# A routed FFN whose expert tiles are gathered through an inverse slot map, and whose shared pieces stand four ahead of the loop and four behind it

## The chip, the cores and the metric
One core of one Trainium2 chip. The metric is the device time of one execution in microseconds. Engines: TensorE (PE), VectorE (DVE), ScalarE (ACT), GpSimd (POOL), SyncE (SP).

## The reference
x has 2 batches of 512 tokens of 512 values. Three layers, each on a layer norm of x:
```
x = x + 0.5 * ffn(layernorm(x))
x = x + attention(layernorm(x))     # 32 heads, 8 key/value heads, head size 128, causal
x = x + 0.5 * ffn(layernorm(x))     # the same weights
ffn(h):
  shared  = (silu(h @ Wg.T) * (h @ Wu.T)) @ Wd.T                  # inner size 512
  probs   = softmax(h @ gate.T)                                   # 16 experts
  w1, w2  = the two largest, divided by their sum
  routed  = w1 * expert_e1(h) + w2 * expert_e2(h)                 # each a gated FFN of inner size 128
  return shared + routed
```

## The kernel before
Everything is float32. A product is split into a high and a low part, high x high + low x high + high x low (PARTS), each float32r; ACT writes the high parts by a copy, DVE or POOL the low parts by a subtraction. The program is written out by hand for each engine, with semaphores between them; each engine works through its list in order.

The tokens are 8 tiles of 128 (TT), two halves of 4. One FFN (`feed_forward(n)`, n = 0 and 1) runs in this order on PE: transposes of the normed half 0 (`turn_norm`), gate/up of shared piece 0, transposes of half 1, `router`, gate/up 1, down 0, `rank`, then for s from 2 to BEFORE-1 gate/up s and down s-1, the transpose of the first expert tile, down BEFORE-1, the loop over expert tiles (`routed`), and the pieces from BEFORE on. The shared FFN is cut into 4 slices of its inner size times 2 halves of the tokens: SLOTS = 8 pieces; a piece is 24 matmuls of gate/up and 12 of down. A slice's weights arrive in `raw_w` and are cut into `wgu` and `wdn`. Down s writes the banks 4 to 7, and `add_down(s)` on DVE adds them to x; a bank is free again only then.

Routing before. DVE's `router` takes softmax, the eight largest and their indices and forms one-hot rows (`hot`, `chosen`). PE's `rank` counts with `below` and `ones` how many tokens ahead chose the same expert. DVE's `place` works out the row of each (token, choice) in a list sorted by expert, each expert padded to whole tiles of 128 (`rows`), and the expert of each of the TILES = 31 tiles, packed six at a time into the integers `tile_w`; it ends with `rows` of the semaphores. Then POOL scatters the 8 tiles of normed tokens twice, 16 indirect DMAs, into `x_rows` in HBM, which was cleared before by a DMA of 31 tiles; SP waits for `scattered` and loads tile after tile (`load_tile`). The experts' weights (16 of 768 KB) are loaded in two groups of eight, ordered among the tile loads; ACT's step waits for the part of them that it needs (`there`).

The loop takes four tiles per iteration, the first iteration and the last written out. `places` reads `tile_w` and works out where in `experts` the weights of six tiles lie. A step j, engine by engine:
- PE: transposes x of tile j+1; transposes `ht` of tile j-1; gate/up of tile j in 12 matmuls, the first three from `tfront`, the other nine from `tback` (wait for `back_lo`); down of tile j-1.
- ACT: `tback_hi` of tile j+1 (768 elements), hT of j-1, `xT_hi`, `tfront_hi` (256 elements), silu of tile j.
- DVE: `xT_lo` and `tfront_lo` of tile j+1, the product `ht` of tile j, the copy of y of tile j-1.
- POOL: `tback_lo` of tile j+1 (768 elements).
- SP: loads tile j+4, stores y of tile j-1 into `y_rows`.

Behind the loop POOL gathers 16 times from `y_rows` into `yg` (two choices for each token tile), and DVE's `combine` adds them with their weights to x: combine 0 between the pieces 6 and 7, combine 2 behind piece 7, combines 4 and 6 behind `add_down(7)`. After the first FFN come `raw_q` and the cuts of attention's weights (`first_cuts` on ACT and POOL: wks, wvs, wqs 0 to 3) and the layer norm of half 0, whose chain on DVE goes `statistics`, ACT's root, `newt` (three steps), `rstd`, the scaling of `xn`; only then PE can transpose and project. After the second FFN the tiles of x are stored, each when it is finished.

## Time and profile before

| | us |
|---|---|
| median of 3 runs | 1210.75 |
| lowest, highest | 1207.58, 1211.01 |
| the profiled execution | 1207.59 |
| its span | 1205.9 |
| first FFN, from the span's start to attention's first projection | 219.8 |
| attention | 784.9 |
| second FFN's loop over expert tiles, and what follows it | 95.2, 33.5 |

The page gives busy time of an engine as a share of the span; a window gives it for a stretch; the chain of waits follows the last instruction back to what released it; a timeline lists instructions in order of time, with the idle time ahead of each and what ended it in square brackets.

### The profile page before, as it was taken

The page shows a single profiled execution, that of the slowest core. Times are in us where ns is not written, and L with a number is a line of the kernel's source. Part 1 is how long each engine was busy: PE and PEld are TensorE (multiplying, and loading weights), DVE is VectorE, ACT ScalarE, POOL GpSimd, SP SyncE. Part 2 cuts the span into 40 slices and gives each one's busy share as a digit, 9 for nine tenths or more (in the row PEclk, how much of TensorE's full clock was granted, in tenths as well). Part 3 has the DMA queues.
Part 4 walks back from the last instruction along what each step waited for, and adds up shares of the span by engine and source line. Part 5 has one row for each costly group of instructions (what it writes and reads, how often), then busy time and mean ns, then how long its engine had stood idle before and what let it go on. Part 6 is the DMA issues. An engine that isn't in the chain of part 4 may idle for free.

```text
span 1205.9 us, 20326 instructions
## 1 busy us (share of the span) xinstructions
PE 1130.7 (94%) x6110; PEld 943.2 (78%) x6111; DVE 701.6 (58%) x1836; ACT 557.6 (46%) x1352; POOL 473.4 (39%) x485
## 2 busy tenths in 40 slices
PE   5989996789999999999999999999999989989994
PEld 4777774678888888888888888888888876877773
DVE  5767776855455545454545454554554556867766
ACT  3336662346435445344544443534553543246650
POOL 1266556116315324323432532531532410365545
PEclk9999998889999999999999999999999999999998
DMA  9986547101101010010010110010100007744546
GB/s 356 346 303 212 161 148 244 53 1 36 53 2 36 9 44 0 35 52 0 35 52 0 35 52 0 35 52 0 35 1 1 1 15 287 301 141 157 160 144 209
DMA packets 38603, 114.62 MB, mean 95 GB/s; under 512 B 4384, under 2 KB 4384, under 8 KB 36512
## 3 DMA queue, kind: packets, MB, share of 16 engines
q1 hardware_dynamic: 33440, 97.30, 22.4%
q0 software_dynamic: 5120, 16.78, 4.1%
q8 instruction: 23, 0.38, 0.1%
q14 instruction: 20, 0.16, 0.0%
HBM read 79.20 MB, written 34.87 MB: 95 GB/s over the span
## 4 chain that ended last, share of the span: by engine, by line
PE 86%; DVE 4%; DMA 3%; issue 2%; ACT 2%; POOL 2%; DVEq 0%; SPq 0%; ACTq 0%; POOLq 0%
PE bank L1221 22%; PE bank L1286 15%; PE bank L1252 10%; PE bank L1298 10%; PE bank L1200 7%; PE bank L1127 6%; PE bank L1234 6%; PE bank L1208 4%; PE bank L1143 2%; POOL yg L484 2%; PE bank L1169 2%; PE bank L1188 1%; PE bank L1100 1%; DMA raw_w<-in_ffn_w 1%; PE bank L1088 1%
## 5 line engine op out<-in xcount | busy, mean ns | idle before, releaser
L498 POOL TENSOR_TENSOR scores<-scores,pinv 128x512 f32<-128x512 f32 (+3 forms) x256 | 176.7, 723 | 378.9 <-DVE pinv L996 378.9
L651 ACT ACTIVATE pT_hi<-bank 128x384 fp32r<-128x384 f32 (+1 forms) x192 | 93.9, 524 | 137.1 <-PE bank L1234 137.1
L450 POOL TENSOR_TENSOR tback_lo<-experts,tback_hi 128x768 fp32r<-128x768 f32 x62 | 115.0, 1857 | 74.4 <-ACT tback_hi L593 73.4
L676 ACT ACTIVATE oT_hi<-bank 128x512 fp32r<-128x512 f32 x64 | 38.3, 599 | 221.5 <-PE bank L1298 221.5
L664 ACT ACTIVATE scores<-scores,nmax 128x512 f32<-128x512 f32 (+3 forms) x256 | 140.3, 557 | 0.3 <-DVE nmax L986 0.3
L966 DVE TENSOR_TENSOR pT_lo<-bank,pT_hi 128x384 fp32r<-128x384 f32 (+1 forms) x192 | 109.5, 598 | 46.9 <-ACT pT_hi L651 46.8
L986 DVE CUSTOM_DVE_ANT_0 scores<-bank,causal 128x512 f32<-128x512 f32 (+3 forms) x256 | 112.2, 486 | 2.2 <-issue 0.2
L970 DVE TENSOR_TENSOR oT_lo<-bank,oT_hi 128x512 fp32r<-128x512 f32 x64 | 44.3, 692 | 112.7 <-ACT oT_hi L676 112.7
L1286 PE MATMUL bank<-wds_hi,oT_hi 128*128 128x512 f32 x256 | 105.5, 412 | 1.4 <-DVE oT_lo L970 1.4
L1221 PE MATMUL bank<-xnT_hi,wqs_hi 128*128 128x512 f32 x256 | 106.7, 417 | 0.0
L1221 PE MATMUL bank<-xnT_lo,wqs_hi 128*128 128x512 f32 x256 | 101.8, 398 | 0.0
L1221 PE MATMUL bank<-xnT_hi,wqs_lo 128*128 128x512 f32 x256 | 101.2, 395 | 0.0
L1286 PE MATMUL bank<-wds_hi,oT_lo 128*128 128x512 f32 x256 | 100.3, 392 | 0.0
L1286 PE MATMUL bank<-wds_lo,oT_hi 128*128 128x512 f32 x256 | 100.0, 391 | 0.0
L1234 PE MATMUL bank<-ident,scores 128*128 128x128 f32 x640 | 90.8, 272 | 2.3 <-DVE pT_lo L966 2.3
L1252 PE MATMUL bank<-kT_hi,qT_hi 128*128 128x512 f32 (+3 forms) x256 | 84.8, 331 | 1.9 <-DVE qT_lo L970 1.9
L1234 PEld LDWEIGHTS bank<-ident,scores 128*128 128x128 f32 x640 | 75.3, 140 | 11.3 <-DVE pT_lo L966 2.8
L1252 PE MATMUL bank<-kT_lo,qT_hi 128*128 128x512 f32 (+3 forms) x256 | 82.6, 323 | 0.0
L1298 PE MATMUL bank<-pT_hi,vv_lo 128*128 128x512 f32 (+3 forms) x256 | 82.6, 323 | 0.0
L1298 PE MATMUL bank<-pT_lo,vv_hi 128*128 128x512 f32 (+3 forms) x256 | 82.3, 321 | 0.0
L1252 PE MATMUL bank<-kT_hi,qT_lo 128*128 128x512 f32 (+3 forms) x256 | 82.2, 321 | 0.0
L1006 DVE TENSOR_TENSOR x<-bank,x 128x512 f32<-128x512 f32 x64 | 44.1, 691 | 64.8 <-PE bank L1286 64.8
(192 smaller groups left out, 2854.0 us busy)
## 6 DMA issues: line engine op xcount, KB each, us to landing
experts<-in_ffn_w SPq DMA_DIRECT2D x32, 768.0 KB, 10.1
xn<-x_rows SPq DMA_DIRECT2D x62, 256.0 KB, 2.7
y_rows<-xn SPq DMA_DIRECT2D x62, 256.0 KB, 2.0
raw_q<-in_wq SPq DMA_DIRECT2D x8, 1024.0 KB, 5.3
raw_d<-in_wd SPq DMA_DIRECT2D x8, 1024.0 KB, 4.8
x_rows<-experts SPq DMA_DIRECT2D x1, 7936.0 KB, 30.0
raw_w<-in_ffn_w SPq DMA_DIRECT2D x8, 768.0 KB, 7.6
raw_kv<-in_wkv SPq DMA_DIRECT2D x8, 512.0 KB, 3.3
```

What stands on the lines that cost most here:

```text
L450: nc.gpsimd.tensor_tensor(tback[par][1][:], experts[:, bass.ds(at + FRONT, GU - FRONT)], tback[par][0][:].bitcast(F32), ALU.subtract).then ...
L498: nc.gpsimd.tensor_tensor(s, s, pinv[k % 2][:, i:i + 1].to_broadcast([P, P * (i + 1)]), ALU.mult).then_inc(att.normed, 1)
L651: nc.scalar.activation(pT[0][:, lo_col:hi_col], bank[b][:, 0:hi_col - lo_col], ACT.Copy).then_inc(att.t_hi, 1)
L664: nc.scalar.activation(s, s, ACT.Exp, bias=nmax[par][:, i:i + 1], scale=-1.0, accum_out=psumr[par][:, i:i + 1]).then_inc(att.exp, 1)
L966: nc.vector.tensor_tensor(pT[1][:, lo_col:hi_col], bank[b][:, 0:hi_col - lo_col], pT[0][:, lo_col:hi_col].bitcast(F32), ALU.subtract).then ...
L986: nc.vector.tensor_tensor_reduce(sp_[par][:, TRI[i]:TRI[i + 1]], bank[bk][:, c:c + w], causal[:, 512 - w:512], -SCORE_SCALE, 3.0e38, ALU.a ...
L1200: last = nc.tensor.matmul(bank[par][:, 0:2 * INTER], xT[par][a][:, c, :], piece[b][:, start:start + FRONT], start=(i == 0), stop=(i == 3 * ...
L1221: last = nc.tensor.matmul(into[:], w[a][:, c, :], xnT[z][:, c, b * SEQ:(b + 1) * SEQ], start=(m == 0), stop=(m == 3 * HC - 1))
L1234: last = nc.tensor.transpose(bank[b][:, at + (i - j) * P:at + (i - j + 1) * P], sp_[par][:, TRI[i] + j * P:TRI[i] + (j + 1) * P], ident[:])
L1252: last = nc.tensor.matmul(bank[bk][:, c:c + P * (i + 1)], qT[a][:, i * P:(i + 1) * P], kT[b][z][:, 0:P * (i + 1)], start=(m == 0), stop=(m ...
L1286: last = nc.tensor.matmul(o_bank(u)[:], oT[ob][h][a][:, tile * P:(tile + 1) * P], wds[h][z][:], start=(m == 0), stop=(m == 3 * G - 1))
L1298: last = nc.tensor.matmul(bank[1][:, j * P:SEQ], vv[bu][a][:, j, :], pT[z][:, COL[j]:COL[j] + SEQ - j * P], start=(j == 0 and m == 0), sto ...
```

## The change
No scatter and no `x_rows`. SP stores the normed tokens as they are into `xn_rows` (two stores of four tiles). `place` ends with two sets of one-hot matrices: `token_hot` (which of the 31 tiles a (token, choice) goes to, which POOL multiplies by the token's number) and `lane_hot` (which lane in the tile). PE's `invert` multiplies them, 16 matmuls of 32 columns, and one more packs the experts of the tiles; DVE's `map_slots` copies the result: `slots`, the token number for each lane of each tile, and `tile_w`. POOL then gathers each expert tile from `xn_rows` with one indirect DMA, four ahead of the loop and then one in each step.

The router's matmuls take high and low gate weights together (2 x 16 columns of weights), 16 in place of 24; the softmax goes, since only the ratio exp(second - first) is needed. `rank` stands ahead of down 0 and uses bank 1. The low part of gate/up slice 1 goes from DVE to POOL. BEFORE is 4 in place of 6. ACT waits once for all 16 experts. In the loop DVE takes the first third of `tback_lo` (`middle`), POOL the rest; POOL's steps are written out. Behind the loop the combines stand ahead of pieces 6 and 7, two pairs each, and the norm of attention waits only for `add_down(6)`; `raw_q` waits for the second pair of gathers. Shared slice 3 is loaded once all gate/up of the loop are done.

```diff
-BEFORE = 6
+BEFORE = 4
@@ SP
+            def store_norm(n, h):
+                part = slice(HALF * h, HALF * h + HALF)
+                sp.wait_ge(norm[2 * n].mul, HALF * (h + 1))
+                sp.dma_start(xn_rows.rearrange("(t p) h -> p t h", p=P)[:, part, :],
+                             xn[:, part, :]).then_inc(route[n].stored, 16)
...
+                load_experts(0, 2)
+                store_norm(n, 0)
+                load_experts(2, 5)
+                store_norm(n, 1)
+                load_shared(n, 2)
+                load_experts(5, NEXP)
                 for k in range(4):
                     store_tile(n, 0, k)
...
+                sp.wait_ge(moe[n].gu_mm, TILES)
+                load_shared(n, 3)
...
-            sp.wait_ge(gathered[HALF - 1], 2 * 16)
+            sp.wait_ge(gathered[HALF // 2 - 1], 4 * 16)
@@ POOL
                 def back(par, at, count):
                     pool.wait_ge(tile_part.back_hi, base + count)
-                    nc.gpsimd.tensor_tensor(tback[par][1][:], experts[:, bass.ds(at + FRONT, GU - FRONT)],
-                                            tback[par][0][:].bitcast(F32),
+                    nc.gpsimd.tensor_tensor(tback[par][1][:, FRONT:], experts[:, bass.ds(at + 2 * FRONT, GU - 2 * FRONT)],
+                                            tback[par][0][:, FRONT:].bitcast(F32),
                                             ALU.subtract).then_inc(tile_part.back_lo, 1)
+                def gather(j):
+                    wait(pool, moe[n].x_mm, j - RING + 1)
+                    nc.gpsimd.indirect_dma_start(
+                        out=xn[:, j % RING, :], out_offset=None, in_=xn_rows,
+                        in_offset=bass.IndirectOffsetOnAxis(ap=slots[:, j:j + 1], axis=0)).then_inc(tile_in[j % RING], 16)
+                pool.wait_ge(route[n].slots, 1)
+                pool.wait_ge(route[n].stored, 2 * 16)
+                for j in range(RING):
+                    gather(j)
+                low_gu(n, BEFORE // 2)
+                pool.wait_ge(route[n].table, 1)
+                back(0, places(pool, 0)[1], 1)
+                low_dn(n, BEFORE // 2)
+                for it in range(TILES // 4 + 1):
+                    at = places(pool, it)
+                    for k in range(4):
+                        j = 4 * it + k
+                        if j + 1 < TILES:
+                            back(1 - k % 2, at[k + 2], j + 2)
+                        if j + RING < TILES:
+                            gather(j + RING)
...
+                low_gu(n, 1)
+                pool.wait_ge(route[n].tokens, 1)
+                flat = token_hot[:].rearrange("p (m t) j -> p m t j", m=2)
+                nc.gpsimd.tensor_tensor(flat, flat.bitcast(F32),
+                                        token[:].unsqueeze(1).unsqueeze(3).to_broadcast([P, 2, TT, TILES + 1]),
+                                        ALU.mult).then_inc(route[n].tokens, 1)
@@ ACT
-                act.wait_ge(route[n].rows, 1)
-                at, there = places(act, 0, loads=True)
-                back(0, at[1], there[1])
-                act.wait_ge(ffn[n].dn_lo, NSH - 1)
+                act.wait_ge(route[n].table, 1)
+                act.wait_ge(m.weights, 16 * NEXP)
+                at = places(act, 0)
+                back(0, at[1])
+                act.wait_ge(ffn[n].dn_lo, BEFORE // 2)
@@ DVE, norm of attention
-                    dve.wait_ge(moe[0].added, 2 * HALF * (h + 1))
+                    dve.wait_ge(ffn[0].added, HALF * (SLOTS - 1 + h))
@@ DVE, place
+                row = rowf[:].rearrange("p m t -> p (m t)")
+                then(nc.vector.tensor_scalar(tile_of[:], row, 1.0 / P, -(P - 1) / (2.0 * P), ALU.mult, ALU.add))
+                then(nc.vector.tensor_scalar(tile_of[:], tile_of[:], ROUNDED, -ROUNDED, ALU.add, ALU.add))
+                dve.wait_ge(s.stored, 2 * 16)
+                nc.vector.tensor_tensor(token_hot[:], counts[:, 0:TILES + 1].unsqueeze(1).to_broadcast([P, 2 * TT, TILES + 1]),
+                                        tile_of[:].unsqueeze(2).to_broadcast([P, 2 * TT, TILES + 1]),
+                                        ALU.is_equal).then_inc(s.tokens, 1)
+                then(nc.vector.scalar_tensor_tensor(out=lane_of[:], in0=tile_of[:], scalar=-float(P), in1=row,
+                                                    op0=ALU.mult, op1=ALU.add))
+                for m in range(2):
+                    nc.vector.tensor_tensor(lane_hot[m][:], counts[:].unsqueeze(1).to_broadcast([P, TT, P]),
+                                            lane_of[:, TT * m:TT * (m + 1)].unsqueeze(2).to_broadcast([P, TT, P]),
+                                            ALU.is_equal).then_inc(s.lanes, 1)
...
+            def map_slots(n, then):
+                s = route[n]
+                dve.wait_ge(s.mapped, 1)
+                nc.vector.tensor_copy(slots[:], bank[1][:, 256:256 + TILES + 1]).then_inc(s.slots, 1)
+                dve.wait_ge(s.exp, 1)
+                then(nc.vector.tensor_scalar(tsum[:], ratio[:], 2.0, 2.0, ALU.mult, ALU.add))
+                then(nc.vector.reciprocal(wtop[:, :, 0], tsum[:]))
+                then(nc.vector.tensor_tensor(wtop[:, :, 1], wtop[:, :, 0], ratio[:], ALU.mult))
+                nc.vector.tensor_copy(tile_w[:], bank[1][0:1, 384:384 + WORDS]).then_inc(s.table, 1)
@@ DVE, loop
+                def middle(par, at, count):
+                    dve.wait_ge(tile_part.back_hi, base + count)
+                    nc.vector.tensor_tensor(tback[par][1][:, 0:FRONT], experts[:, bass.ds(at + FRONT, FRONT)],
+                                            tback[par][0][:, 0:FRONT].bitcast(F32),
+                                            ALU.subtract).then_inc(tile_part.middle_lo, 1)
...
                     if exists(j, 0, TILES - 2):
+                        middle(1 - par, at[k + 2], j + 2)
                         turned(1 - par, j + 2)
                         front(at[k + 2], j + 2)
@@ DVE, feed_forward
                 then = router(n)
-                shared(n, 1, 2)
+                multiply(n, 1)
                 place(n, then)
-                shared(n, 2, BEFORE)
+                shared(n, 1, 2, multiplied=True)
+                shared(n, 2, 3)
+                map_slots(n, then)
+                shared(n, 3, BEFORE)
                 routed(n)
-                shared(n, BEFORE, SLOTS - 1)
+                shared(n, BEFORE, SLOTS - 2)
                 combine(n, 0)
+                combine(n, 2)
+                shared(n, SLOTS - 2, SLOTS - 1)
+                combine(n, 4)
+                combine(n, 6)
                 shared(n, SLOTS - 1, SLOTS)
-                combine(n, 2)
...
             add_down(0, SLOTS - 1)
-            combine(0, 4)
-            combine(0, 6)
@@ PE
                 wait(pe, f.mul, s - 1)
+                if s == 3:
+                    pe.wait_ge(route[n].table, 1)
...
+            def invert(n):
+                s = route[n]
+                pe.wait_ge(s.tokens, 2)
+                for m in range(2):
+                    pe.wait_ge(s.lanes, m + 1)
+                    for t in range(TT):
+                        i = TT * m + t
+                        last = nc.tensor.matmul(bank[1][:, 256:256 + TILES + 1], lane_hot[m][:, t, :], token_hot[:, i, :],
+                                                start=(i == 0), stop=(i == 2 * TT - 1), skip_group_check=True)
+                pe.wait_ge(s.expert_of, 1)
+                pe.wait_ge(consts.packing, RING + 2)
+                nc.tensor.matmul(bank[1][0:1, 384:384 + WORDS], tilef[:], packing[:], start=True, stop=True,
+                                 skip_group_check=True).then_inc(s.mapped, 1)
...
                 gate_up(n, 1)
+                rank(n)
                 down(n, 0)
-                rank(n)
                 for s in range(2, BEFORE):
                     gate_up(n, s)
+                    if s == 2:
+                        invert(n)
                     down(n, s - 1)
```

## Rows read from the trace of the kernel before

**Rows 1.** The page, span and engines: busy us (share of the span), instructions
```profile
span 1205.9 us, 20326 instructions
...
PE 1130.7 (94%) x6110; PEld 943.2 (78%) x6111; DVE 701.6 (58%) x1836; ACT 557.6 (46%) x1352; POOL 473.4 (39%) x485
```

**Rows 2.** Windows: stretch, length, busy us of each engine, granted clock, DMA share, GB/s
```profile
87.20:181.15 93.95, 89.57 (x564) 68.75 (x564) 67.52 (x118) 62.22 (x147) 52.58 (x29) 1.00 0.53 181
202.40:219.80 17.40, 3.67 (x16) 3.27 (x16) 15.53 (x23) 6.07 (x10) 10.96 (x11) 0.61 0.66 254
1005.00:1022.60 17.60, 15.10 (x84) 10.25 (x82) 13.18 (x30) 9.01 (x16) 2.35 (x1) 1.00 0.96 386
1172.40:1205.90 33.50, 17.49 (x74) 13.39 (x72) 19.09 (x29) 2.46 (x4) 16.21 (x16) 0.84 0.64 204
```

**Rows 3.** Chain of waits, first FFN ahead of the loop: start us, us, what
```profile
26.46 5.58 PE bank L1100 x24
...
33.12 5.80 PE bank L1127 x24
...
41.90 1.69 PE bank L1158 x16
...
49.29 2.75 PE bank L1143 x12
```

**Rows 4.** Timeline of DVE, routing: start, us, line, instruction, output<-input, count, [idle before]
```profile
38.96 0.29 DVE L826 TENSOR_TENSOR chosen<-hot 128x128 f32<-128x128 f32 x1
...
40.10 1.23 DVE L868 TENSOR_TENSOR wgu_lo<-raw_w,wgu_hi 128x1024 fp32r<-128x1024 f32 x1 [0.26 <-ACT wgu_hi L550]
...
41.85 2.48 DVE L887 SCALAR_TENSOR_TENSOR x<-bank,x 128x512 f32<-128x512 f32 x4
...
45.63 0.42 DVE L843 TENSOR_REDUCE ahead<-wide 128x16 f32<-128x256 f32 x1
...
47.95 0.71 DVE L853 TENSOR_TENSOR wide<-counts,upto 1x544 f32<-1x544 f32 x1
```

**Rows 5.** Timeline of all engines, one iteration of the first loop
```profile
137.01 0.33 PE L1188 MATMUL bank<-ident,ht 128*128 128x128 f32 x1 [0.59 <-DVE ht L931]
...
138.78 0.41 DVE L921 TENSOR_TENSOR tfront_lo<-experts,tfront_hi 128x256 fp32r<-128x256 f32 x1
...
146.09 0.85 ACT L593 ACTIVATE tback_hi<-experts 128x768 fp32r x1 [1.01 <-issue]
...
147.25 1.82 POOL L450 TENSOR_TENSOR tback_lo<-experts,tback_hi 128x768 fp32r<-128x768 f32 x1 [2.05 <-ACT tback_hi L593]
...
148.23 1.12 DVE L921 TENSOR_TENSOR tfront_lo<-experts,tfront_hi 128x256 fp32r<-128x256 f32 x1
...
149.60 0.33 PE L1188 MATMUL bank<-ident,ht 128*128 128x128 f32 x1 [0.60 <-DVE ht L931]
```

**Rows 6.** Timeline of all engines, from the first loop's end towards attention
```profile
185.61 0.98 POOL L484 DMA_INDIRECT yg<-y_rows,rows  x1 [9.29 <-DMA y_rows<-xn]
...
186.90 0.96 POOL L484 DMA_INDIRECT yg<-y_rows,rows  x1 [0.30 <-issue]
...
199.36 2.73 DVE L959 SCALAR_TENSOR_TENSOR x<-yg,wtop,x 128x512 f32<-128x512 f32 x4
...
206.00 7.42 DVE L768 TENSOR_TENSOR newt<-root 128x4 f32<-128x4 f32 x1 [0.71 <-ACT root L526]
...
208.48 4.91 POOL L505 TENSOR_TENSOR wqs_lo<-raw_q,wqs_hi 128x512 fp32r<-128x512 f32 x4
...
214.72 3.67 PE L1088 MATMUL bank<-ident,xn 128*128 128x128 f32 x16 [12.35 <-DVE xn L773]
```

**Rows 7.** Windows of PE alone: stretch, length, busy us, granted clock, DMA share, GB/s
```profile
198.50:202.40 3.90, 3.87 (x10) 0.56 0.92 322
246.00:256.50 10.50, 8.44 (x30) 0.52 0.00 0
1189.20:1192.20 3.00, 2.99 (x12) 1.00 0.83 231
```

292 lines of the change are left out of this document (115 added, 177 removed).

## The prediction

> **What bounds the kernel now.** The page comes first: TensorE (PE) is busy 1130.7 of a span of 1205.9 us [rows 1], so only about 75 us can be won without taking matmuls away. The windows say where PE is not busy: little in the attention stage, 16.0 us in the tail behind the last expert tile, 13.7 us in the passage from the first FFN to attention, 4.4 us in the first loop over expert tiles [rows 2]. The chain of waits gives the price of each piece of PE work [rows 3], the timelines of the engines the order behind each idle spot [rows 4 to 6]. Attention's code is untouched and priced at nothing. The kernel has two FFNs, so every FFN term counts twice. The sum is made against the profiled execution, 1207.59 us (span 1205.9 and 1.7 around it); the median of the three runs lies 3.2 us above it. About 0.3% (3.6 us) is what a measurement of this kernel can tell from no change.
>
> I follow the path in three parts: up to the end of the last gate/up before the loop, the loop, and what follows it.
>
> **Part 1, routing against fewer pieces.** A piece costs PE 5.6 (gate/up) plus 2.75 (down), 8.35 us [rows 3]. BEFORE 6 to 4 takes two out of this part: -16.7. The routing then has to fit into less work, and it grows.
> - Router: 24 matmuls in 5.58 become 16, 1.9 less [rows 3]; but two ACT copies of 0.6 that queue behind the first piece's activation gate the transposes, so I count 1.1: gate/up 1 starts at 32.0, not 33.1.
> - Router chain on DVE: the softmax and its small steps go, an addition of the halves comes; `chosen`, now ready at 39.2 [rows 4], comes 3 us earlier and before PE needs it. Hidden.
> - `rank` now stands ahead of down 0 and starts when gate/up 1 ends, 37.8, and takes 1.7 to 1.9 [rows 3]: DVE's `place` starts at 39.75. At 39.0 POOL starts the low part of gate/up 1, 2.4 us, formerly DVE's 1.23 [rows 4]. Its second and third instructions find it busy. How that goes the loop shows: `tfront_lo`, both inputs in SBUF, takes 0.41 alone and 1.12 when POOL's `tback_lo` is under way, ending 0.28 after it [rows 5]; one of four elements took 7.42, as long as POOL's cuts behind one another [rows 6]. So `place` stands until 41.35: 1.2 lost.
> - Then by the nearest rows (0.2 for a small one, 0.42 to 0.46 for 256 elements, 0.71 for 544, 1.23 for 1024 [rows 4]): 3.1 to `tile_of`, 0.7 for `token_hot`, then two `lane_hot` of 1.23 on DVE and POOL's multiply of 512 elements, 1.23 as its cuts in [rows 6], all needing both inputs from SBUF and so one after another: 3.7. Last 0.8 for the expert of each tile. End about 49.7, ranging 48.4 (the 0.8 beside POOL) to 51.
> - PE after `rank`: down 0 and gate/up 2, done at 48.05. `invert` is 17 small matmuls; `rank`'s 16 take 1.69 [rows 3]; half of them wait for the lanes. It ends at 49.9, and down 1 waits further for the low part and the first add, to 51.0: about 3 us lost with `invert` itself. Down 1 ends at 53.75.
> - Gate/up 3 waits for `table`, which DVE writes only after the low part (0.6), add 0 (2.48 [rows 4]), multiply 2, an ACT copy, low part 2 (2.0 in all), add 1 (2.48), low down (0.6) and `map_slots` (1.0): 49.7 + 9.1 = 58.8. PE is idle 5.05 us from 53.75. This is the largest new wait. Gate/up 3 ends at 64.4, against 74.4 for gate/up 5 now: **-10.0** per FFN instead of -16.7.
> - Clock: after pauses the granted clock falls. The row after a 2.1 us pause shows 0.56, one in attention's start 0.52 over 10.5 us, half speed being 1.2 GHz; after 2.3 us at 1186.9 it stayed 1.00 [rows 7]. The transposes behind 12.35 us of idleness took 3.67 [rows 6]. Five idle microseconds behind one more lie nearer the first kind: I take 4 us of matmuls at half speed, **+2.0** per FFN; bounds 0 and 5 (the 10.5 us stretch).
> - DMA: gone are the 7.9 MB clear and 16 scatters per FFN, come two stores of 1 MB. ACT now waits for all 16 experts, the last 11 issued near 29 us behind DVE's first low down. The row of such loads shows 386 GB/s [rows 2]; 12 loads of 0.79 MB take 24.5 us and end near 55, needed at 66 (second FFN: 11 us of room). SP stands on `stored` sources and that low part meanwhile; queued behind it are only loads with room. Cost nothing; without that room every late microsecond would count.
>
> **Part 2, the loop.** One iteration of four tiles takes 12.59 us, from one PE transpose of `ht` to the same four later [rows 5]. It is not PE's 2.84 per tile that sets it but this ring: ACT `tback_hi`, POOL `tback_lo` (1.82), DVE `tfront_lo` 0.28 behind POOL, DVE `ht`, PE, and ACT again; two tiles take 5.9 us, and once per iteration ACT stands 1.01 for the registers of `places`, 0.84 more than else [rows 5]: 5.9 + 5.9 + 0.8 = 12.6.
> The change takes a third from POOL's piece (1.82 to 1.23), gives DVE `middle` (0.41), and puts a gather behind POOL's piece, 0.96 and 0.30 of issue [rows 6]. POOL per tile: 0.3 + 1.23 + 0.3 + 1.0, 2.83 to 2.9; with `places` 0.47 per iteration, 11.9. Everything hangs on who takes the port first. POOL's piece used to start 0.15 to 0.3 us before DVE was free; now the gather keeps POOL until after DVE has started `middle`, and that repeats itself, since the loop is entered so. PE then sees 2.85 per tile and 3.45 at the boundary: 12.0. 25 intervals at 0.15 less (the last four have no gather): -3.7, of which I keep **-3.0** per FFN, for gathers that take 1.44 at times. Bounds: -5 (PE's own rate), +6 (POOL first: `middle` waits for it, two tiles 6.25 and 13.3 per iteration). The loop's entry is taken as now, -0.25. The gathers themselves are issued three tiles ahead and hidden.
>
> **Part 3, behind the loop.** PE has four pieces, 33.5 us, in place of two, 16.7. POOL's 16 gathers begin 4.4 us behind the loop's end and take 1.26 each [rows 6], landed by 27: now covered. But DVE is late. From the multiply of piece 5 (11.3 us behind the loop's end): low gate/up and add 4 to 16.55, two pairs of combines (2.73 per four [rows 6]) to 21.95, piece 6 and add 5 to 26.95, two more pairs to 32.35, piece 7's multiply, ACT copy and low part to 34.35, add 6 to 36.75. Down 7 can start at 34.95, PE having been idle 4.2 us. Second FFN: add 7 ends at 39.2 (full clock) to 40.9 (half), then 2.45 to the end as now: 41.65 to 43.35, I take 42.5. Now it is 33.5 [rows 2]: **+9.0**.
> First FFN: statistics from add 6, root 3.2 later, 40.3 us; ACT then cuts `wqs` 1 to 3 and POOL follows at 40.85 with three cuts of 1.23. The chain `newt`... `rstd` needs 0.8 and its last step, both inputs in SBUF, comes at 40.9. In the row now `newt` stood until the last of six cuts [rows 6], so I let it stand until 44.6, then 5.7 to the first projection as now, half-speed transposes included (0.7 behind the end of `newt` to 219.8 [rows 2, 6]), and 0.1 for the rest of the chain. 50.4 against 38.65 (181.15 to 219.8): **+11.7**; bounds +8.1 (it slips through) and +12.2.
> Here a page bears on it. The Trainium skill, SBUF — State Buffer, Who interferes with whom, says that a DVE instruction with two SBUF inputs contends with a GpSimd one that reads SBUF, and that `tensor_scalar` in a 2-port mode contends too. The first half the trace shows, 7.42 us [rows 6]; for the second no row has POOL beside the scaling of `xn`. By that rule +11.7 would hold even if `rstd` slipped through, without it +8.1 would be reached.
>
> **Sum.** First FFN: -10.0 + 2.0 - 0.25 - 3.0 + 11.7 = +0.45. Second: -10.0 + 2.0 - 0.25 - 3.0 + 9.0 = -2.25. Together -1.8: 1207.6 - 1.8 = 1205.8 on the profiled execution's level, 1209 on the median's.
>
> **Rivals.**
> A, more is hidden (0.27): pauses do not lower the clock (-4 to -5), the `wqs` cuts let `rstd` by (-3.6), the loop runs at PE's rate (-4). All: -14; two of them: 1197 to 1205. For it: 2.3 us left the clock alone [rows 7]. Against: the pause here is double.
> B, POOL first, slower (0.17): in the loop POOL's piece starts ahead of `middle`. Place: `tback_lo` against DVE's `y_out` copy; it decides once POOL is free more than 0.4 us earlier than I have it (a gather of under 0.6, or its issue beside the previous piece). Up to +9 per FFN against my -3; in half of the iterations +9 in all: 1218, in all 1227.
> C, the routing takes longer (0.12): `place` stuck behind POOL twice more, or half speed as long as the 10.5 us stretch: +3 to +6 over both: 1213 to 1216.
> D, POOL bound (0.06): DVE's holds and gathers of 1.44 make POOL 3.1 per tile, gain gone: 1215.
> The forecast, within 1204 to 1213, has 0.38.
>
> **Chances.** Faster than 1207.1: all of A and a third of the forecast's case, 0.40. Slower than 1214.4: B, most of C and D, 0.28. Within: 0.32. The range must leave out 0.2: the best corner of A (0.1) and the worst of B (0.1): 1197 to 1220.
>
> **What the new profile would show.** Right: PE idle about 5 us ahead of gate/up 3, ended by DVE's `tile_w`; loop iterations near 12.0 us with `middle` at 0.41; no scatter rows; no wait of PE for gathers; in the tail a PE wait of about 4 us ahead of down 7, ended by the low part; a long `newt` or `rstd` beside POOL's cuts. Wrong: `middle` of 1.2 to 1.6 us and iterations of 13 (B), a clock of 1.00 throughout the routing (A), ACT waiting for the experts' DMA at the loop's entry, `place` longer than 10 us (C).

## The result, and the profile after

The changed kernel took 1224.7 us (median of 4, 1224.62 to 1227.68), the kernel before 1209.2: ratio 1.0136, interval 1.0111 to 1.0161. It is slower by 15.5 us, and lies above the range of the forecast (1197 to 1220). The profiled execution has a span of 1222.9 us against 1205.9.

The same program ran twice more in the study, beside variants: 1216.75 us (e0_changed_again, ratio 1.0087, 1.0069 to 1.0105) and 1223.61 us (e12_changed_third, ratio 1.0146, 1.0105 to 1.0186). So it has two levels, the high one in two sessions and the low one in a third. The kernel before stood at 1206.9, 1207.2, 1208.5 and 1207.9 in the four sessions of the study; against the kernel before beside it the changed kernel was 15.5, 9.5 and 15.8 us slower, so the levels are some 6 us apart (7 to 8 us in its own time: the kernel before was itself 1 to 2 us longer in the sessions of the high level). What tells them apart is shown below; the lower one is nearer to what the change itself costs.

The page of the changed kernel, span and busy time of each engine, answers to [rows 1]:

```profile
span 1222.9 us, 20118 instructions
...
PE 1142.8 (93%) x6130; PEld 952.0 (78%) x6131; DVE 740.9 (61%) x1890; ACT 556.2 (45%) x1352; POOL 476.8 (39%) x526
```

PE is busy 12.1 us more, with only 20 matmuls more. The windows (columns as in [rows 2]; first loop, its tail up to attention, second loop, its tail):

```profile
79.41:174.17 94.76, 92.07 (x565) 70.38 (x566) 86.03 (x147) 62.21 (x147) 62.66 (x54) 0.98 0.47 153
174.17:229.24 55.07, 42.53 (x163) 32.14 (x161) 37.28 (x62) 13.26 (x22) 24.93 (x24) 0.88 0.49 170
1076.29:1174.23 97.94, 92.16 (x565) 70.34 (x566) 85.22 (x147) 62.11 (x147) 61.24 (x54) 0.99 0.45 148
1174.23:1222.90 48.67, 37.45 (x146) 28.03 (x144) 28.42 (x43) 6.27 (x10) 16.14 (x16) 0.92 0.50 157
```

The last column but two is the granted clock: 0.88 and 0.92 in the tails. Ahead of the loops and behind them PE's busy time grew by 12.4 us, mostly from matmuls at the lower clock; the loops added 4.1, and attention gave 4.4 back. Of idleness the two tails hold 12.5 and 11.2 us. Read from one landmark of PE's timeline to the next, the time of the three profiles divides so (us; "again" is e0_changed_again; the tile 1 of a loop is the first that has the full ring around it):

| stretch | forecast of the difference | before | changed | again |
|---|---|---|---|---|
| start to the end of the last gate/up ahead of the loop | -8.0 | 74.4 | 65.1 | 63.6 |
| to the gate/up of tile 1 | -0.25 | 12.6 | 14.3 | 14.3 |
| to the first piece behind the loop | -3.0 | 94.2 | 94.8 | 94.6 |
| to attention's first projection | +11.7 | 38.7 | 55.1 | 51.1 |
| attention, to the second FFN's first gate/up | 0 | 789.4 | 785.7 | 785.9 |
| to the end of the last gate/up ahead of the loop | -8.0 | 55.5 | 47.1 | 48.0 |
| to the gate/up of tile 1 | -0.25 | 12.6 | 14.3 | 14.3 |
| to the first piece behind the loop | -3.0 | 95.2 | 97.9 | 99.1 |
| to the end of the span | +9.0 | 33.5 | 48.7 | 43.2 |

The terms ahead of the loop came near the forecast. The loop and its entry did not; the tails did in the run again, and not in the first profile; attention gave 3.6 us that nobody had counted.

**Routing.** Rows of the changed kernel's timelines, first DVE's, then PE's:

```profile
38.94 1.49 DVE L819 TENSOR_SCALAR ntile<-ntile 128x16 f32<-128x16 f32 x1
...
44.26 3.22 DVE L840 TENSOR_TENSOR lane_hot<-counts,lane_of 128x1024 fp32r<-128x1024 f32 x2
...
56.86 0.15 DVE L858 CAST tile_w<-bank 1x8 int32<-1x8 f32 x1
```

```profile
46.96 1.85 PE L1180 MATMUL bank<-token_hot,lane_hot 128*128 128x32 f32 x16
48.74 0.20 PE L1184 MATMUL bank<-packing,tilef 128*1 128x8 f32 x2
49.58 0.47 PE L1152 MATMUL bank<-wdn_hi,ab_hi 128*128 128x512 f32 x1 [0.64 <-DVE x L882]
...
57.16 0.77 PE L1136 MATMUL bank<-xnT_hi,wgu_hi 128*128 128x512 f32 x1 [4.58 <-DVE tile_w L858]
```

`place` starts at 38.7; its second step takes 1.49 us in place of 0.17, because POOL's low part of gate/up 1 runs beside it (the 1.2 us of the forecast). `invert` runs at 46.96, PE waits 0.64 for add 0, and 4.58 for `tile_w` ahead of gate/up 3 (forecast 5.05), which then starts at half clock and takes 8.0 us in place of 5.8. In the run again this wait is 3.12 us and gate/up 3 takes 7.4.

**The first level: signals that come late.** In the tail PE, ACT and POOL read so, in the changed kernel's first profile:

```profile
191.09 0.40 PE L1136 MATMUL bank<-xnT_hi,wgu_lo 128*128 128x512 f32 x1
...
197.84 0.40 PE L1136 MATMUL bank<-xnT_lo,wgu_hi 128*128 128x512 f32 x1 [0.57 <-issue]
198.55 0.40 PE L1136 MATMUL bank<-xnT_hi,wgu_lo 128*128 128x512 f32 x1 [0.31 <-issue]
```

```profile
183.18 0.60 ACT L559 ACTIVATE sg<-bank 128x512 f32<-128x512 f32 x1 [1.38 <-issue]
...
201.36 0.60 ACT L559 ACTIVATE sg<-bank 128x512 f32<-128x512 f32 x1 [13.74 <-remote]
```

and in the run again:

```profile
189.84 0.60 ACT L559 ACTIVATE sg<-bank 128x512 f32<-128x512 f32 x1 [3.89 <-PE bank L1136]
```

The matmul at 191.09 is the last of the gate half of piece 6. ACT's silu waits for its signal and for nothing else, and starts at 201.36, 9.9 us after that matmul has ended; the bracket can name no releaser ("remote"; at 183.18 "issue"). PE goes on to piece 7 and then stands 0.3 us ahead of matmul after matmul without a wait of its own. In the second FFN the silu is 7.9 us late. In the run again it starts 0.05 us behind its matmul and the bracket names PE. Each late silu pushes DVE's multiply, the adds and the last down behind it: against the run again the two tails are 4.0 and 5.4 us longer. POOL issues its 16 gathers meanwhile, in both runs; here in the first profile:

```profile
190.74 0.94 POOL L473 DMA_INDIRECT yg<-y_rows,rows  x1 [0.30 <-issue]
...
198.40 0.95 POOL L473 DMA_INDIRECT yg<-y_rows,rows  x1 [0.30 <-issue]
```

### The profile page after: what moved, and what is told of

It reads as the page before. It is cut to its first block and busy times, and to the rows that moved or that the text cites. A ratio compares the mean times of both kernels' runs of the same rounds, so it can differ in the third digit from the quotient of the medians.

```text
span 1222.9 us, 20118 instructions
## 1 busy us (share of the span) xinstructions
PE 1142.8 (93%) x6130; PEld 952.0 (78%) x6131; DVE 740.9 (61%) x1890; ACT 556.2 (45%) x1352; POOL 476.8 (39%) x526
## 5 line engine op out<-in xcount | busy, mean ns | idle before, releaser
L426 POOL TENSOR_TENSOR tback_lo<-experts,tback_hi 128x512 fp32r<-128x512 f32 x62 | 82.8, 1336 | 50.3 <-ACT tback_hi L583 46.6
L1276 PE MATMUL bank<-kT_lo,qT_hi 128*128 128x512 f32 (+3 forms) x256 | 82.5, 322 | 0.0
```

The costliest lines, as they stand in the source:

```text
L426: nc.gpsimd.tensor_tensor(tback[par][1][:, FRONT:], experts[:, bass.ds(at + 2 * FRONT, GU - 2 * FRONT)], tback[par][0][:, FRONT:].bitcast( ...
L1276: last = nc.tensor.matmul(bank[bk][:, c:c + P * (i + 1)], qT[a][:, i * P:(i + 1) * P], kT[b][z][:, 0:P * (i + 1)], start=(m == 0), stop=(m ...
```

## The experiments

Four sessions of four runs, each with the kernel before beside it. Medians, ratios to the kernel before with their intervals:

| run | us | ratio | interval |
|---|---|---|---|
| e1_tail_order | 1215.77 | 1.0080 | 1.0051 to 1.0109 |
| e2_plain_loads | 1213.69 | 1.0056 | 1.0031 to 1.0080 |
| e3_middle_on_pool | 1210.73 | 1.0028 | 1.0010 to 1.0046 |
| e4_table_early | 1204.67 | 0.9984 | 0.9967 to 1.0002 |
| e0_changed_again | 1216.75 | 1.0087 | 1.0069 to 1.0105 |
| e5_six_ahead | 1224.74 | 1.0149 | 1.0128 to 1.0169 |
| e6_early_and_entry | 1206.07 | 0.9992 | 0.9982 to 1.0003 |
| e7_early_and_order | 1203.90 | 0.9988 | 0.9972 to 1.0003 |
| e8_late_cuts | 1223.68 | 1.0132 | 1.0096 to 1.0167 |
| e9_middle_first | 1229.81 | 1.0189 | 1.0158 to 1.0220 |
| e10_combined | 1201.53 | 0.9948 | 0.9926 to 0.9970 |
| e11_before_late_cuts | 1204.75 | 0.9972 | 0.9952 to 0.9992 |
| e12_changed_third | 1223.61 | 1.0146 | 1.0105 to 1.0186 |
| e13_late_cuts_again | 1222.50 | 1.0121 | 1.0083 to 1.0158 |
| e14_plain_tail | 1217.47 | 1.0081 | 1.0055 to 1.0108 |
| e15_combined_again | 1203.34 | 0.9960 | 0.9939 to 0.9982 |

The first eight had their signals on time: apart from the first piece of each FFN, every silu starts within 0.1 us of the end of its gate half. The last eight, e14 aside, had late ones, as in the first profile of the changed kernel. Late were only silus whose gate half ended after POOL had begun ten or more indirect DMAs in a row: with four begun, and in e11 with nine, the silu of the same profile was on time. Only runs of the same kind are compared below. The sessions are e1 to e4; e0, e5, e6 and e7; e8 to e11; e12 to e15. The first, third and fourth ran on the same chip, so the late signals don't belong to a chip. A comparison across sessions (e1 to e4 beside e0) comes out alike by the ratios, within 1.1 us.

**e1_tail_order.** DVE's order behind the loop as before.

```diff
-                shared(n, BEFORE, SLOTS - 2)
-                combine(n, 0)
-                combine(n, 2)
-                shared(n, SLOTS - 2, SLOTS - 1)
-                combine(n, 4)
-                combine(n, 6)
-                shared(n, SLOTS - 1, SLOTS)
+                shared(n, BEFORE, SLOTS - 1)
+                combine(n, 0)
+                shared(n, SLOTS - 1, SLOTS)
+                combine(n, 2)
...
             add_down(0, SLOTS - 1)
+            combine(0, 4)
+            combine(0, 6)
...
```

The waits of the norm, the adds and the stores that belong to this order are as before too.

> DVE's order behind the loop as in the kernel before: combine 0 between the pieces 6 and 7, combine 2 behind piece 7, combines 4 and 6 at the very end; norm and stores wait as before. All else as in the changed kernel (1224.7). Theory S (a stall while POOL issues gathers: PE's signals of piece 6, ended at 191.5, reach ACT at 201.3, and PE itself stutters from 197.8 to 201.3): the order of DVE's work has nothing to do with it; ACT's silu of piece 6 is again some 8 to 10 us late, and the time falls by what DVE's queue costs alone, the 4.9 us of PE's wait ahead of down 7 and a part of the combines, 2 to 8 us: 1217 to 1223. Rival Q (DVE's late work is the cause of all of it): the silu of piece 6 comes at once, and each FFN gains 8 to 12 us: 1202 to 1208.

The silu of piece 6 came at once, but it also did in e2, e3 and e4, which have the changed kernel's tail: Q's sign proves nothing. Beside e0 it is 1.0 us, no difference, and both ranges were missed. The tails are 49.6 us (e0: 51.1) and 45.8 to the span's end (43.2): the new order of the combines costs 1.5 in the first FFN and gives 2.6 in the second.

**e2_plain_loads.** No gathers in the loop.

```diff
@@ POOL
-                for j in range(RING):
-                    gather(j)
...
-                        if j + RING < TILES:
-                            gather(j + RING)
@@ SP, in each step
+                        load_tile(n, it + 1, k)
                         store_tile(n, it, k)
```

`load_tile` copies 128 neighbouring rows of `xn_rows` in place of the tile's own, so the routed products are those of other tokens.

> The expert tiles are no longer gathered by POOL; SP loads them with plain DMAs, one per tile and three ahead as before, from fixed rows of xn_rows (so the tiles hold other tokens; the table and slots are still worked out and waited for). The 16 gathers behind the loop stay. Theory S1 (the gathers in the loop leave something behind that later stalls the signals in the tail): the silu of piece 6 is on time, 8 to 10 us less per FFN, 1205 to 1210, the loop near 12.0 to 12.4 us per four tiles. Rival S2 (only the 16 gathers of the tail matter, while PE is at work beside them): the stall stays, the loop gives 0 to 3 us per FFN, 1218 to 1225. Third (gathers keep DVE waiting in the loop, `middle` at 1.5 us by POOL's gathers): iterations fall from 12.46 to 11.9.

1213.7, 3.1 us under e0, between the ranges of S1 and S2; the two intervals overlap, so the total can't be told from e0's. The loops' iterations are 12.3 (e0: 12.47) and 12.94 us (12.96), not the 11.9 of the third theory. So the forecast's idea that the gathers set when POOL's piece starts is wrong: without them `middle` is still held up, 1.07 and 1.17 us in the mean of the two loops (e0: 1.15 and 1.20), against 0.41 alone. The gathers aren't free, though: in the profiles each loop is 1.5 us shorter without them and each entry 0.7. What hides it in the sum is attention, 789.4 us against 785.9, with a stretch at half speed that e0 has not (last section).

**e3_middle_on_pool.** No `middle`.

```diff
-                        middle(1 - par, at[k + 2], j + 2)
...
-                middle(0, at[1], 1)
...
-                    nc.gpsimd.tensor_tensor(tback[par][1][:, FRONT:], experts[:, bass.ds(at + 2 * FRONT, GU - 2 * FRONT)],
-                                            tback[par][0][:, FRONT:].bitcast(F32),
+                    nc.gpsimd.tensor_tensor(tback[par][1][:], experts[:, bass.ds(at + FRONT, GU - FRONT)],
+                                            tback[par][0][:].bitcast(F32),
                                             ALU.subtract).then_inc(tile_part.back_lo, 1)
```

> The whole low part of `tback` (768 elements) is POOL's again, DVE has no `middle`; the gathers stay in the loop. Theory L (the loop's ring is set by DVE behind POOL, and `middle` at 0.41 or 1.5 us depending on who starts first only moves the wait): iterations 12.6 to 13.2, +1 to +4 us per FFN, 1226 to 1232. Rival (POOL bound, 1.82 + 0.96 + 0.6 of issue = 3.4 per tile): iterations 13.6, +8 per FFN, 1240. Second rival (`middle` blocked is the loss): 12.2, 1221.

1210.7, 6.0 us faster than e0. The first two theories had it slower and are wrong. The second rival (`middle` blocked is the loss) had the direction, 3.7 us faster than the 1224.7 of its time, but not the place: it wanted iterations of 12.2. They are 12.55 us in both FFNs (0.1 more than e0 in the first, 0.4 less in the second), and the entry is 12.4 us where e0 has 14.3. The share of `tback_lo` that moved to DVE is a loss.

**e4_table_early.** One function moved on DVE.

```diff
                 shared(n, 1, 2, multiplied=True)
+                map_slots(n, then)
                 shared(n, 2, 3)
-                map_slots(n, then)
```

> `map_slots` one piece earlier on DVE, right behind add 0 and ahead of multiply 2; nothing else. Theory T (PE's 4.58 us ahead of gate/up 3 are DVE's queue ahead of `tile_w`, and nothing behind it absorbs them): `tile_w` at 52.4 in place of 57.0, gate/up 3 starts at 52.4, and what the half clock after the pause costs (some 2 us) goes too: -4.5 to -7 per FFN, 1211 to 1216. Rival (the loop's entry waits for the experts' weights or for POOL, so that most of it comes back there): -1 to -2 per FFN, 1221 to 1223.

1204.7, 12.1 us faster than e0, 6 per FFN: theory T. Gate/up 3 starts at 53.3 and takes 5.8 us in place of 7.4 to 8.0. Here the tail from the loop's end to the projection is 50.7 us, to the span's end 43.2, against 50.4 and 42.5 forecast.

**e0_changed_again.** No edit.

> The changed kernel itself, beside others of this study. All four variants of it so far had the silu of piece 6 right behind its gate matmuls, with the same tail in three of them, where the changed kernel's profile had it 8 to 10 us late in both FFNs. Theory K (the stall belongs to this very program, where its instructions and signals fall): it is there again, and the time is 1220 to 1225. Rival R (it belonged to the chip or the session of those four executions): it is gone, the tails are 50.7 and 43.2 us after the loop's end, and the time is 1212 to 1216.

1216.75, no late silu: R. The change without late signals costs 9.5 us; the other 6 go with them (between the two profiles the tails differ by 9.4).

**e5_six_ahead.** e1 with BEFORE = 6, slice 3 loaded ahead of the loop.

```diff
-BEFORE = 4
+BEFORE = 6
@@ SP
                 load_experts(5, NEXP)
+                load_shared(n, 3)
...
```

> The changed kernel with BEFORE = 6 and DVE's order behind the loop as in the kernel before: the new routing and the gathers alone, without the new split. Theory P (routing costs 7.4 us more per FFN ahead of the loop once no pieces are moved: gate/up 3 still waits 4.6 us for `tile_w`; the loop and the tail are those of before): 1216 to 1222, that is the split by itself is worth nothing or a small gain beside e1_tail_order (1215.8). Rival (the two more pieces hide the wait and the entry): 1205 to 1210.

1224.7: 17.5 us above the kernel before, and above the ranges of theory and rival. The last gate/up ahead of the loop ends at 82.5 us (before: 74.4), the entry takes 14.2, and the loops (95.25 and 95.27 against 94.2 and 95.2) and their tails (38.5 and 34.3 against 38.7 and 33.5) are within 1.1 us of before. So the new routing, the gathers and `middle` lose 17.5 us, and moving two pieces behind the loop gives 9.0 of it back (e1 against e5): the split is worth something, the routing isn't.

**e6_early_and_entry, e7_early_and_order.** On top of e4: POOL's low part of gate/up slice 2 moved behind the loop's last piece; and e1's order.

```diff
@@ e6, POOL
-                low_gu(n, BEFORE // 2)
                 pool.wait_ge(route[n].table, 1)
...
+                pool.wait_ge(tile_part.front_lo, base + TILES)
+                low_gu(n, BEFORE // 2)
```

> e4_table_early with one more edit: POOL makes the low part of gate/up slice 2 behind its last piece of the loop (once DVE has written the last `tfront_lo`), not ahead of the loop's first `tback_lo`. Theory E (at the loop's entry that low part of 2.38 us holds up DVE's `ab_lo` of piece 3, 2.46 us instead of 0.69, and POOL's own first `tback_lo`; PE's waits of 1.73 and 3.9 us there are its consequence): the entry becomes 2 to 4 us shorter per FFN, 1197 to 1201 against 1204.7. Rival (the entry is set by the chain add 2, middle, front, add 3 on DVE alone): -0.5 or nothing; and at the loop's end it may block DVE: 0 to +2.

> e4_table_early with DVE's order behind the loop as in the kernel before (as e1_tail_order). Theory Q2 (the order of the combines matters by the tails alone: 49.6 against 50.7 us in the first FFN, 45.8 against 43.2 in the second): +1.5 us, 1205 to 1207.5. Rival (it was what freed e1_tail_order of the stall, worth 9 us): with no stall here, no difference, 1204 to 1205.

e6: the entry became 12.5 us in both FFNs (from 14.3), as theory E has it, but 1206.1 is no gain over 1204.7. What went is PE's wait of 1.7 us ahead of down 3; the one of 3.9 us for `ht` stayed. Of the 1.8 us in the first FFN 0.7 are gone again at the next tile (5.09 us where e4 has 4.38), and in the profile attention took 789.3 us where e4 has 786.1, again with a half-speed stretch that e4 has not. The sum stays within what can be told apart. e7: 1203.9, 0.8 below e4, Q2 and its rival can't be told apart.

**e9_middle_first.** The order that the forecast had assumed.

```diff
-                    pool.wait_ge(tile_part.back_hi, base + count)
+                    pool.wait_ge(tile_part.middle_lo, base + count)
```

> The changed kernel, POOL's `tback_lo` waits for DVE's `middle` of the same tile (which itself waits for ACT's high part). This forces the order that the forecast assumed. Theory N (`middle` beside or behind POOL's piece, 1.5 us in place of 0.41 on two tiles of four, makes these tiles 3.34 to 3.39 us instead of 2.83 to 2.95): iterations of 11.8 to 12.0 in both FFNs, -3 us in the first and -6 in the second, 1207 to 1209. Rival (the wait only moves on to `tfront_lo`, which then ends 0.28 behind a POOL piece that starts 0.4 later): 12.4 to 12.9, 1214 to 1218.

The rival in the iterations: 12.76 and 12.91 us, against 12.47 and 12.97 in e8_late_cuts of the same session. The entry came down from 14.3 to 12.8 us, PE's wait for `ht` there from 3.9 to 2.3. Both ranges were missed: the median is 1229.8 us, 6.1 above e8. The profiled execution took 1221.95, the other five 1229.5 to 1232.1, so what made those five longer is in no trace, and only the iterations are read here. Why they did not get shorter, three kernels show. The changed kernel, timeline of DVE:

```profile
111.61 1.51 DVE L921 TENSOR_TENSOR tback_lo<-experts,tback_hi 128x256 fp32r<-128x256 f32 x1
...
115.22 0.42 DVE L921 TENSOR_TENSOR tback_lo<-experts,tback_hi 128x256 fp32r<-128x256 f32 x1 [0.36 <-ACT tback_hi L583]
...
116.21 0.86 DVE L927 TENSOR_TENSOR tfront_lo<-experts,tfront_hi 128x256 fp32r<-128x256 f32 x1
...
117.89 1.64 DVE L921 TENSOR_TENSOR tback_lo<-experts,tback_hi 128x256 fp32r<-128x256 f32 x1
```

Line 921 is `middle`, 927 `tfront_lo`. POOL's piece takes 1.3 us and begins within 0.1 us of `middle`, since ACT's high part releases both (POOL's rows at 115.23 and 117.93). On some tiles `middle` gets in first (0.42) and `tfront_lo` is held up (0.86), on the others `middle` is held up (1.51, 1.64). Of 24 tiles in the middle of the first loop `middle` is short on 6, and those are the ones with a long `tfront_lo`; in the second loop POOL has the better of all 24, and `middle` takes 1.20 us in the mean. POOL's rows for the same tiles:

```profile
111.55 1.30 POOL L426 TENSOR_TENSOR tback_lo<-experts,tback_hi 128x512 fp32r<-128x512 f32 x1 [0.98 <-ACT tback_hi L583]
...
115.23 1.56 POOL L426 TENSOR_TENSOR tback_lo<-experts,tback_hi 128x512 fp32r<-128x512 f32 x1 [1.27 <-ACT tback_hi L583]
116.94 0.97 POOL L433 DMA_INDIRECT xn<-xn_rows,slots  x1
117.93 1.30 POOL L426 TENSOR_TENSOR tback_lo<-experts,tback_hi 128x512 fp32r<-128x512 f32 x1
```

Twice of three times POOL waited for ACT, 0.98 and 1.27 us, with nothing of its own in the way; the third piece follows its gather at once. With the order forced, e9, timeline of all engines:

```profile
116.89 0.41 DVE L921 TENSOR_TENSOR tback_lo<-experts,tback_hi 128x256 fp32r<-128x256 f32 x1
...
117.61 1.29 POOL L426 TENSOR_TENSOR tback_lo<-experts,tback_hi 128x512 fp32r<-128x512 f32 x1 [0.61 <-DVE tback_lo L921]
...
118.19 0.99 DVE L927 TENSOR_TENSOR tfront_lo<-experts,tfront_hi 128x256 fp32r<-128x256 f32 x1
```

`middle` is short on every tile, POOL's piece starts later, and `tfront_lo` takes 0.98 to 1.37 us on 47 of the 48 such tiles. Without `middle`, e3:

```profile
109.16 1.85 POOL L426 TENSOR_TENSOR tback_lo<-experts,tback_hi 128x768 fp32r<-128x768 f32 x1
...
110.33 0.96 DVE L927 TENSOR_TENSOR tfront_lo<-experts,tfront_hi 128x256 fp32r<-128x256 f32 x1
```

`tfront_lo` again 0.96. DVE has two instructions per tile in place of one that don't run at their own speed beside POOL's piece, and on each of these tiles one of them meets it.

**e8_late_cuts, e12_changed_third, e13_late_cuts_again, e11_before_late_cuts.**

```diff
-            first_cuts(low_part)
+            first_cuts(low_part, 0, 3)
+            pool.wait_ge(norm[1].mul, HALF)
+            first_cuts(low_part, 3)
```

> The changed kernel, with POOL's low parts of `wqs` 1 to 3 held back until the four tiles of the norm of half 0 are scaled. Theory V (of the first FFN's tail, 51.1 us in the changed kernel run again, 1.1 us are `rstd` and 2.9 us are the scaling of `xn`, 4.22 against 1.3 for four tiles alone, both beside POOL's three cuts; the half clock behind the pause stays): tail 47.0 to 47.6, time 1212.5 to 1213.5. Rival (only instructions with both inputs in SBUF are held up, the scaling is slow for itself): -1.1, 1215.6. Second rival (the projections then wait for the late cuts): 1216 or more.

> The changed kernel once more, beside three variants, because it ran at two levels so far: 1224.7 with PE's signals to ACT some 9 us late in both tails, and 1216.75 without. Theory H (it is a condition of the session that the executions share, not of the program): it is at one of these two levels, and its trace tells which by the start of the silu of piece 6, 2.8 or 12 us behind the start of its gate matmuls, and the variants beside it follow.

> e8_late_cuts again, now to be read against the changed kernel of the same session. Theory V as before: -3.3 to -4 us beside e12_changed_third, the tail of the first FFN 47.0 to 47.6 if the signals are on time. Rival (the half clock or later projections eat it): 0 to -1.

> The kernel before with the late cuts of `wqs` alone: `newt` took 7.42 us there, six cuts long; with the last three held back it ends with the third cut at 209.7 instead of 213.4, and `xn` is scaled without POOL beside it: -3.7 to -4.3 us, 1203. Rival (PE's first projections wait for the late cuts, or the clock falls lower behind the shorter pause): -1 or nothing.

e12 bears H out: 1223.6, the silu of piece 6 7.1 us behind the start of its gate matmuls in both FFNs, where 3.0 is on time. That is 4.2 us late, not the 9.9 of the first profile, and yet the tails are as long (54.9 and 48.5 us): piece 7's silu starts at 203.2 us in e12, 203.8 in the first profile and 198.2 in e0, and the tails follow that one. e13 beside e12: the first FFN's tail 50.7 us against 54.9, -4.2, theory V as to the tail. DVE's rows of e0 and of e13:

```profile
214.70 1.25 DVE L764 TENSOR_TENSOR rstd<-newt,root 128x4 f32<-128x4 f32 x1
215.99 4.22 DVE L766 TENSOR_SCALAR xn<-x,mv,rstd 128x512 f32<-128x512 f32 x4
```

```profile
221.24 0.16 DVE L766 TENSOR_TENSOR rstd<-newt,root 128x4 f32<-128x4 f32 x1
221.43 1.92 DVE L768 TENSOR_SCALAR xn<-x,mv,rstd 128x512 f32<-128x512 f32 x4
```

In e0 POOL's three low parts lie beside DVE's four scalings, and PE waits 3.34 us for them, POOL first and then PE:

```profile
214.67 3.89 POOL L494 TENSOR_TENSOR wqs_lo<-raw_q,wqs_hi 128x512 fp32r<-128x512 f32 x3 [2.73 <-ACT wqs_hi L619]
```

```profile
208.98 0.77 PE L1152 MATMUL bank<-wdn_hi,ab_hi 128*128 128x512 f32 x1 [5.31 <-DVE x L882]
...
217.49 0.90 PE L1096 MATMUL bank<-ident,xn 128*128 128x128 f32 x3 [3.34 <-DVE xn L766]
```

With the cuts behind the scalings `rstd` went from 1.25 to 0.16 us, the four scalings from 4.22 to 1.92 (1.91 in the kernel before, not the 1.3 of the expectation). But the time fell by 1.1 us only (1222.5 against 1223.6, no difference that can be told), as the rival had it. In the profiles most of it went in attention. The windows show e13 and then the changed kernel at the same distance from the first projection:

```profile
254.10:264.20 10.10, 7.99 (x26) 6.06 (x25) 3.37 (x5) 2.65 (x5) 1.11 (x3) 0.50 0.00 0
```

```profile
257.30:267.50 10.20, 7.58 (x47) 6.29 (x45) 5.15 (x16) 3.41 (x7) 1.19 (x3) 1.00 0.00 0
```

The granted clock is 0.50 (1.2 GHz) for 10.1 us in e13, as in the kernel before [rows 7], and 1.00 in the changed kernel. Attention takes 788.7 us in e13 and e8, 785.7 in e12. In the changed kernel a half-speed stretch begins within the pause of 3.9 us (222.3 to 232.5, in PE's transposes and the first projections). Whether the late cuts cause the stretch in attention is not shown: e15, which has them, has none (last section). The kernel before with the late cuts takes 1204.75 against 1208.54, ratio 0.9972: a gain of 0.3% whose interval just leaves out 1, though DVE waited 4.05 us for `root` there, 0.71 in the kernel before.

**e14_plain_tail.** The 16 gathers of the tail replaced by 16 plain DMAs of the same size.

> The changed kernel, but `yg` is filled by 16 plain DMAs of SP from consecutive tiles of `y_rows` instead of POOL's 16 gathers (so the rows added to x are others; `rows` is still worked out). Theory G (where signals come late in the tail, POOL's indirect DMAs beside PE's work are what delays them): if e12 shows late signals, this one does not, and takes 1210 to 1215; if e12 shows none, it takes 1215 to 1217, a little less than e12, since nothing waits for the gathers there. Rival (any heavy DMA traffic does it): the silu is as late as in e12.

Beside e12, same session. ACT's silu of piece 6, e12 first:

```profile
195.66 0.60 ACT L559 ACTIVATE sg<-bank 128x512 f32<-128x512 f32 x1 [8.01 <-remote]
```

```profile
191.45 0.60 ACT L557 ACTIVATE sg<-bank 128x512 f32<-128x512 f32 x1 [3.89 <-PE bank L1134]
```

Late with the gathers, on time without, though the same 4.2 MB are moved. Tails of 50.1 and 43.1 us (e12: 54.9 and 48.5), 1217.5 against 1223.6 us: theory G as to the signals; its range of 1210 to 1215 was missed. The profiled execution of e14 took 1212.9 us, one of two at this level, the other four 1217.1 to 1218.9; whether signals were late in those four no trace tells. e11 has the same sign at another place, while POOL issues its scatters beside PE's shared pieces: the last matmul of piece 5's gate half ends at 69.97. ACT and POOL of e11:

```profile
72.58 0.60 ACT L569 ACTIVATE sg<-bank 128x512 f32<-128x512 f32 x1 [3.67 <-remote]
```

```profile
68.44 0.96 POOL L473 DMA_INDIRECT x_rows<-xn,rows  x1 [0.30 <-issue]
69.70 0.96 POOL L473 DMA_INDIRECT x_rows<-xn,rows  x1 [0.30 <-issue]
```

The silu starts at 72.58, 2.6 us late, and the bracket again has no releaser. What late signals cost in the loop can't be seen: e12's and e14's iterations (12.47 and 12.96 us) are those of e0.

**e10_combined, e15_combined_again.** e4, e3 and e8 together.

> The changed kernel with `map_slots` a piece earlier (e4), the whole `tback_lo` on POOL (e3) and the late cuts of `wqs` (e8). If the gains add: -12 (e4) - 6 (e3) - 3.5 (e8) from 1216.75: 1195. Rival (after the early table the loop's entry is in the way again, so e3's gain at the entry is part of e4's): 1199 to 1202.

> e10_combined again, which took 1201.5 in a session in which e8_late_cuts had late signals in both tails. If the signals are on time: 1194 to 1198 (tails 47 and 40.7 us). If they are late again: 1201 to 1202.

1201.5 and 1203.3 (0.9948 and 0.9960; expected were 1199 to 1202 by the rival, and 1201 to 1202): faster than both kernels, in sessions with late signals (piece 6's silu 7.1 us behind the start of its gate matmuls in the first FFN of both, 5.7 and 9.3 in the second). From 1223.6 of the changed kernel that is 20 to 22 us. What it takes with signals on time wasn't run.

## Why the prediction was wrong

The forecast was 1209, faster or equal in 0.72 of its chances; measured were +15.5 us, of which +9.5 came without late signals; the rest goes with them. The profiled spans differ by +17.0 where the sum had -1.8. Loops and entries account for 13.3 of the gap (forecast -6.5, measured +6.8), late signals in the tails for 9.4 and the tails besides for 1.5; part 1 was 1.7 better than forecast and attention 3.6.

**Right: part 1.** -8.0 forecast, -9.3 and -8.4 measured (-10.8 and -7.5 in e0). The largest new wait was named with its releaser and its length (5.05, measured 4.58, in e0 3.12), the half clock behind it too (+2.0, measured 2.2 and 1.6), `place` beside the low part (1.2, measured 1.3), the experts' loads covered.

**Right: the tails, with signals on time.** +11.7 and +9.0 forecast, +12.4 and +9.7 measured in e0, PE's wait ahead of down 7 at 5.3 and 4.4 (forecast 4.2), though the last to end it was add 6, which frees the banks, and not the low part. Inside the first tail the size was right partly by luck: the sum let `newt` stand for 3.6 us, but it came before POOL's cuts and slipped through (0.16 us); `rstd` lost 1.1 and the scalings 2.3 in its place. That is the case for which the page on SBUF was quoted. POOL beside the scaling of `xn` makes four of them 4.22 us, alone they take 1.92. This agrees with what the Trainium skill, SBUF — State Buffer, Who interferes with whom, says of a `tensor_scalar` in a 2-port mode; that the scaling runs in such a mode no row tells.

**Wrong: "the gather keeps POOL until after DVE has started `middle`, and that repeats itself", -3.0 per FFN.** Measured +0.6 and +2.8 (e0: +0.4 and +3.9). Two steps failed. POOL is mostly not kept by the gather but released by ACT's `tback_hi`, at the same moment as `middle` (e2: without gathers the iterations are 0.17 and 0.02 us shorter, not 0.5). And with `middle` first, as e9 forced it, the iteration is 12.8 us, not 12.0, because I let `tfront_lo` pass beside a POOL piece that had just begun. Rival B had the right place and the wrong alternative: it treated POOL first as the bad case, with up to +9 per FFN, while either order holds up one instruction, by 0.4 to 1.3 us; with POOL first on all tiles, in the second loop, it was +2.8.

**Wrong: "The loop's entry is taken as now, -0.25".** +1.7 per FFN. There DVE is behind already (add 2, add 3) and got `middle` twice more in front of the product that PE waits for. e0's rows at the entry, DVE and then PE:

```profile
65.35 2.46 DVE L901 TENSOR_TENSOR ab_lo<-sg,ab_hi 128x512 fp32r<-128x512 f32 x1 [0.92 <-ACT ab_hi L564]
...
71.40 2.47 DVE L882 SCALAR_TENSOR_TENSOR x<-bank,x 128x512 f32<-128x512 f32 x4
73.78 1.30 DVE L921 TENSOR_TENSOR tback_lo<-experts,tback_hi 128x256 fp32r<-128x256 f32 x1
...
75.61 1.90 DVE L927 TENSOR_TENSOR tfront_lo<-experts,tfront_hi 128x256 fp32r<-128x256 f32 x1
```

```profile
77.76 0.48 PE L1212 MATMUL bank<-ident,ht 128*128 128x128 f32 x1 [3.92 <-DVE ht L938]
```

`middle` takes 1.30 us beside POOL's piece, `tfront_lo` 1.90, and PE's wait for `ht` is 3.9 us in place of 2.25. Without `middle` (e3) it is 2.05, with `middle` first (e9) 2.3: the hold-up of `middle` is what the entry lost.

**Wrong: "Attention's code is untouched and priced at nothing".** -3.6 us. A half-speed stretch that the kernel before has inside attention [rows 7] is gone in this profile; 1.6 of the 3.6 us come in the first two groups of heads, where it lay. That part is no sure doing of the change, since profiles of other variants of it have the stretch (last section). The other 2 us are some 0.15 us in each of the other groups: 47.80 us a group in the changed kernel and all its variants, 47.95 in the kernel before and e11. So they belong to the program; their cause is open.

**Not foreseen: the late signals,** +4.0 and +5.4 in the tails of the first profile. The sum took the signals' way at nothing. Without them 1216.75 lies within the range, on the wrong side of the forecast.

**Where the expected gain went.** Two pieces moved are 16.7 us of PE work per FFN that stand behind the loop instead of ahead. What they free there is eaten by the routing (e5: +8.1 to the last gate/up with six ahead), above all by `tile_w`, which was written behind a piece's work that could wait (e4: 6 us per FFN for moving one function); and behind the loop DVE, not PE, sets the end, so that four pieces cost there 9.7 to 12.4 us more than two.

## What to carry to other kernels

When work moves from one engine to another, count the instructions that are held up beside the other engine, not their microseconds alone: cutting POOL's piece by 0.55 us (1.85 to 1.30) and giving DVE 0.41 made one more of them, and lost. When a wait is new, look at what stands ahead of its releaser in that engine's queue; here one function placed one call too late cost 12 us, more than the 9.5 us that the whole change lost. A half-speed stretch far from the edit can hide what an edit gained (e2, e6, e13): compare stretches and granted clock over the whole span, not the edited stage alone.
